# A three-layer decoder on one core: in the second layer the attention product reaches feature layout by DMA, not by TensorE transpositions

## The reference, cut to what matters

```python
x = _layernorm(x + attn(x))            # causal, 16 heads of 16 features
x = _layernorm(x + xattn(x, ctx))      # cross attention with a key mask
x = _layernorm(x + ffn(x))             # attention without mask, plus a mixture of 8 experts, 2 of them used
# in each attention: softmax(q k^T / 4) v, heads side by side; in the first two a projection W_o and a bias follow
```

## Time and profile before

| | |
|---|---|
| median of three executions | 923.28 us (922.69 to 924.7) |
| profiled execution | 925.48 us, its span 923.7 us |
| busy: PE, PEld | 94%, 80% of the span |
| busy: DVE, ACT, POOL | 84%, 63%, 46% |
| DMA | 109 GB/s mean |

### The profile page before, as it was taken

One profiled execution on the slowest core, in us unless ns is written; L12 is line 12 of the kernel. 1 busy time (PEld: TensorE's weight loads), 2 busy tenths in 40 slices (PEclk: granted clock), 3 DMA queues, 4 the chain that ended last, 5 costly groups with the idle time before them and its releaser, 6 DMA issues.

```text
span 923.7 us, 28634 instructions
## 1 busy us (share of the span) xinstructions
PE 872.9 (94%) x9988; PEld 741.6 (80%) x9988; DVE 774.2 (84%) x3718; ACT 582.9 (63%) x1211; POOL 427.7 (46%) x588
## 2 busy tenths in 40 slices
PE   7798999989889999999999999999999999999996
PEld 4688888878778888888888778888888888888874
DVE  3689898988978888888898878888888888888885
ACT  4578777877777887878787644444444444445433
POOL 7588787878775453535445323222222222222201
PEclk8999999999999999999999999999999999999999
DMA  6565565545444453444434222222222222222210
GB/s 176 158 174 166 136 174 150 158 143 166 127 111 133 114 154 95 132 113 117 118 109 112 71 71 71 82 82 82 82 81 82 82 82 82 82 81 78 66 35 24
DMA packets 98165, 100.49 MB, mean 109 GB/s; under 512 B 10701, under 2 KB 90599, under 8 KB 98023
## 3 DMA queue, kind: packets, MB, share of 16 engines
q1 hardware_dynamic: 97159, 97.87, 38.3%
q10 hardware_dynamic: 864, 0.79, 0.4%
HBM read 18.14 MB, written 4.19 MB: 24 GB/s over the span
## 4 chain that ended last, share of the span: by engine, by line
PE 71%; ACT 8%; issue 8%; DMA 5%; DVE 4%; POOL 2%; SPq 2%; ACTq 0%; POOLq 0%; DVEq 0%
PE work L517 39%; PE work L661 9%; PE scores L638 8%; PE max_scores L614 7%; DMA q_stack<-neg_max_t 4%; PE work L670 3%; PE scores L641 3%; ACT attn L827 2%; PE work L542 1%; SPq L443 1%; ACT x_all L849 1%; DVE max_scores L993 1%; ACT neg_max_t L821 1%; DMA q_stack<-q_parts 1%; PE work L704 1%
## 5 line engine op out<-in xcount | busy, mean ns | idle before, releaser
L993 DVE CUSTOM_DVE_ANT_0 max_scores<-max_scores,mask_qk 128x128 f32<-128x128 f32 x992 | 253.3, 324 | 36.1 <-PE max_scores L614 35.7
L827 ACT ACTIVATE attn<-scores 128x512 f32<-128x512 f32 x384 | 214.9, 595 | 74.2 <-PE scores L638 68.3
L638 PE MATMUL scores<-q_stack,k_stack 128*128 128x128 bf16 x1536 | 144.6, 220 | 21.8 <-DMA q_stack<-neg_max_t 10.8
L614 PE MATMUL max_scores<-k_stack,q_stack 126*128 126x128 bf16 x1536 | 148.7, 221 | 5.8 <-DMA q_stack<-q_parts 3.6
L1107 POOL TENSOR_TENSOR q_full<-q_full,q_parts 128x512 f32<-128x512 f32 x48 | 55.9, 1164 | 192.9 <-ACT q_parts L779 192.9
L993 DVE DVE_READ_ACCUMULATOR2_ANT neg_max<- 128x1 f32 x992 | 138.8, 140 | 0.0
L638 PEld LDWEIGHTS scores<-q_stack,k_stack 128*128 128x128 bf16 x1536 | 97.0, 97 | 44.1 <-DMA q_stack<-neg_max_t 17.2
L614 PEld LDWEIGHTS max_scores<-k_stack,q_stack 126*128 126x128 bf16 x1536 | 99.1, 98 | 41.4 <-issue 22.8
L1066 DVE SCALAR_TENSOR_TENSOR x_all<-work,combine,x_all 128x256 f32<-128x256 f32 x256 | 122.6, 479 | 7.5 <-PE work L517 2.8
L517 PE MATMUL work<-split_hi,w_hi 128*128 128x256 f32 x384 | 115.7, 301 | 4.5 <-DVE split_lo L896 4.4
L517 PE MATMUL work<-w_hi,split_hi 128*128 128x256 f32 (+2 forms) x320 | 113.6, 355 | 0.0
(11 more groups left out here) (125 smaller groups left out, 2073.8 us busy)
## 6 DMA issues: line engine op xcount, KB each, us to landing
q_stack<-q_parts SPq DMA_DIRECT2D x288, 128.0 KB, 2.4
k_stack<-k_parts SPq DMA_DIRECT2D x282, 128.0 KB, 2.4
in_t<-in_xt SPq DMA_DIRECT2D x16, 256.0 KB, 3.0
x_all<-in_x SPq DMA_DIRECT2D x16, 256.0 KB, 3.2
in_t<-in_ct SPq DMA_DIRECT2D x16, 256.0 KB, 2.8
out<-x_all SPq DMA_DIRECT2D x16, 256.0 KB, 2.2
stage<-in_e SPq DMA_DIRECT2D x4, 512.0 KB, 4.7
stage<-in_qk SPq DMA_DIRECT2D x2, 512.0 KB, 4.1
```

The lines of the kernel that those rows point to most:

```text
L614: mm = pe.matmul(dst[:, b, h2, :], head(QS, n, 2 * p + h2, b, ROWS), head(KS, n, 2 * p + h2, b, ROWS), start=(b + h2 == 0), stop=(b + h2 = ...
L638: mm = pe.matmul(dst[:, b, h2, :], head(KS, n, 2 * p + h2, b, rows), head(QS, n, 2 * p + h2, b, rows), start=(b + h2 == 0), stop=(b + h2 = ...
L827: act.activation(attn("exp", n, p)[:, :, :], SS[g % 2][:, :, :, :].rearrange("k b h q -> k (b h) q"), ACT.Exp).then_inc(probs_done, 1)
L993: ins = dve.tensor_tensor_reduce(scores, scores, MQ[l][:, :], -1.0, HUGE, ALU.add, ALU.min, NM[n % 2][:, b, h:h + 1])
```

## The change: what it does

In the second layer (`MOVED = (1,)`):

- `VA` holds 32 columns for each head in all layers, feature and one in turn (feature 0, one, feature 1, one, ...). So the product with v has features on the even rows and the sum on each odd row. The halves of the pairs are laid out so that a row holds 512 values that make up two rows of the feature layout.
- `zd` (SyncE, for each half f): a DMA of the 64 even rows (128 KB) into `ZC[:, f, :]`, and a DMA of one sum row for each of four heads-in-a-quad (8 KB) into `ZS[:, f, :]`, spread over 128 lanes, 16 values in each.
- `rz` (VectorE): the reciprocal of `ZS` (128 x 32) and its split in three bf16 parts, five small instructions, each waiting for the one before.
- `rd` (SyncE): three DMAs that gather each part (8 KB, 128 pieces of 64 bytes) into 8 rows of `RT`.
- `bc` (PE): two bf16 matmuls with a selecting matrix `SEL`, 24 rows deep and 256 columns wide, which spread each reciprocal over the features of its head. `z` is then one multiplication of 128 x 512 on VectorE, in place in `ZC`.
- `zT` and `zt` are gone in this layer. `zh` and `zl` read `ZC` in SBUF and not PSUM. `zd` of the next item waits for `zl`.
- The weights and biases are permuted on the host, the constants have one more load (128 KB) and one more cast, and the memset of `VA` grows from 574 to 1024 values per lane for each buffer.
- All due times of all three layers are new. The order of PE around `maxt` in the second layer is now: `s2` (seventh, eighth), `s1` (eighth), `xt`, `pv` (second half), `v`, `maxt`, `q`, `s1`, `s1`, `s2` (first), `s2`, `s1`, `k`, `s2`, `s2`, `bc`. On VectorE: `nm`, `xl`, `rz`, then the eight `max` of the next item with `cl`, `z`, `zl` and `sum` between them. On SyncE: `zd` (second half), `ml`, `rd`, then `qs`. On ScalarE `za` (second half) comes straight after the last `exp`.

```diff
-VH = DH + 1
-V_COLS = (H - 1) * VH + QUAD
+V_COLS = H * QUAD
+MOVED = (1,)
-PERIOD = [16.53, 18.13, 24.97]
+PERIOD = [16.52, 18.01, 25.02]
 ...
+     "z": [23.59], "in": [-69.69], "ch": [-49.91], "cl": [-48.7], "xt": [-41.93], "xh": [-40.53], "xl": [-38.82],
+     "res": [-0.26], "zh": [24.2], "zl": [24.69], "out": [26.33], "sum": [28.38], "rs": [35.67], "norm": [44.58],
+     "va": [-12.54], "zd": [8.35, 14.21], "rz": [17.38], "rd": [14.91], "bc": [23.06]},
 ...
+            def move_z(n, f):
+                sp.wait_ge(za_done[f], n + 1)
+                if n:
+                    sp.wait_ge(zl_done, n)
+                src = attn("za", n, f)
+                sp.dma_start(ZC[:, f, :], src[0:P:2, :, :]).then_inc(z_moved[f], 16)
+                sp.dma_start(ZS[:, f, :], src[1:P:QUAD, :, :]).then_inc(z_moved[f], 16)
+
+            def move_recips(n, part):
+                sp.wait_ge(recip_done, moved(n))
+                if moved(n) > 1:
+                    sp.wait_ge(bc_psum, moved(n) - 1)
+                for j in range(PARTS):
+                    sp.dma_start(RT[8 * j:8 * j + 8, :], RP[j][:, :, :]).then_inc(recip_moved, 16)
 ...
-                            o, h = QUAD * (2 * b + h2), 8 * f + 2 * p + h2
-                            mm = pe.matmul(dst[o:o + QUAD, p * P:(p + 1) * P], VA[n % VALUES][:, b, h * VH:h * VH + QUAD],
+                            h, half = 8 * f + 2 * p + h2, p // 2
+                            o, u = QUAD * (2 * (p % 2) + h2), 2 * half + b
+                            mm = pe.matmul(dst[o:o + QUAD, u * P:(u + 1) * P], VA[n % VALUES][:, b, h * QUAD:(h + 1) * QUAD],
 ...
+            def broadcast_recips(n, part):
+                pe.wait_ge(recip_moved, PARTS * 16 * moved(n))
+                dst = mine("bc", n)
+                recips = RT[0:8 * PARTS, :].rearrange("r (m f e) -> r m f e", f=2, e=P // 8)
+                for f in range(2):
+                    mm = pe.matmul(dst[:, f * TOK:(f + 1) * TOK], SEL[0:8 * PARTS, :], recips[:, :, f, :], start=True, stop=True)
+                mm.then_inc(bc_psum, 1)
 ...
             def z_tokens(n, f):
+                if layer(n) in MOVED:
+                    for g in range(2):
+                        dve.wait_ge(z_moved[g], 2 * 16 * moved(n))
+                    dve.wait_ge(bc_psum, moved(n))
+                    z = ZC[:, :, :].rearrange("p c t -> p (c t)")
+                    dve.tensor_tensor(z, bank("bc", n)[:, :], z, ALU.mult).then_inc(zq_done, 1)
+                    return
 ...
+            def sum_recips(n, part):
+                for g in range(2):
+                    dve.wait_ge(z_moved[g], 2 * 16 * moved(n))
+                if moved(n) > 1:
+                    dve.wait_ge(recip_moved, PARTS * 16 * (moved(n) - 1))
+                link(dve.reciprocal(ZS[:, :, :], ZS[:, :, :]))
+                for j in range(PARTS - 1):
+                    link(dve.tensor_copy(RP[j][:, :, :], ZS[:, :, :]))
+                    ins = dve.tensor_tensor((ZS if j < PARTS - 2 else RP[j + 1])[:, :, :], ZS[:, :, :], RP[j][:, :, :], ALU.subtract)
+                    if j < PARTS - 2:
+                        link(ins)
+                ins.then_inc(recip_done, 1)
 
             def z_low(n, part):
                 dve.wait_ge(zh_done, n + 1)
+                if layer(n) in MOVED:
+                    dve.tensor_tensor(ZL[:, :, :], ZC[:, :, :], ZH[:, :, :].bitcast(F32), ALU.subtract).then_inc(zl_done, 1)
+                    return
```

127 lines of the change are left out of this document (84 added, 43 removed), and 61 rows, old and new, of tables (SHIFTS, TIMES).

## The result

The changed kernel takes 946.28 us (median of four executions, 942.04 to 953.86) against 922.99 (922.07 to 924.7) before: a ratio of 1.0249, interval 1.0208 to 1.0291. Slower, as forecast, but by 23 us instead of 4, and outside the range of 914 to 939. The four executions lie at 942.0, 943.7, 948.9 and 953.9; the profiled one is that of 943.71, with a span of 941.9.

A forecast was written before the change was run, and what follows sets the result against it. PE's instructions were taken to bound the second layer; its saving would go to waits at `ml` and `rz`. 15 cycles x 0.2 us plus 0.7 for the start gave +3.7, 927.0 us from 923.28; range 914 to 939.

The forecast's parts named there:

- The usual cycle: Second layer, `maxt` to `maxt`: 16.2 us a cycle, 0.2 more than now.
- PE's wait there: PE before the first `s2`, for the DMA `ml`: stands still 0.97 us instead of 0.20.
- `bc` comes at: PE reaches `bc` about 6.8 us after `maxt`, just in time for the last `rd` DMA, landing at 6.9 (8.1).
- surplus: VectorE's `zl`, with both inputs now in SBUF: 0.15 to 0.3 us more, bounds 0 and 1.0.
- The price of `rz`: Five linked VectorE instructions on 128x32: 1.07 us, bounds 1.07 and 3.4.
- One cycle was taken for all: Sum over the second layer: 15 cycles x 0.2 us = 3 us.
- 12.7 of 16 us: SyncE's issuing in a cycle: some 8.4 us now, 12.7 with seven more issues at 0.61 each.
- Whatever is late here has no cover: PE at `bc`: at the long end of the `rd` landing, PE and VectorE lose over a microsecond once more.
- Rival C: Clearly slower: DMAs with 64-byte pieces take 3.6 us or more, `bc` late too; cycle some 17.0 us, 938 to 940; chance 0.15.
- The start: Longer `VA` memset before PE's warm-up, one more load and cast: +0.7 us, between -1 and +2.
- From the first `maxt` of the first layer to the first of the second: First layer, same instructions in a new order: 0 us, between -2 and +3.
- 3.2 + 12.7 + 0.46: VectorE's cycle: `rz` ends 3.2 us after `maxt`, 12.7 to `nm`, 0.46 for `nm` and hand-over; given as 16.3 us.

The follow-up runs named there:

- experiment 9: Changed kernel without the sums' DMAs, `rz`, `rd`, `bc` and `z`, plus idle reciprocals on VectorE before the first `max` of four items: 939.14 us.
- experiment 10: Changed kernel without sums, `rz`, `rd`, `bc`, `z`, with ScalarE's `norm` after the last `exp`: 921.28 us; additionally k earlier 930.41, or v before second `pv` 937.83.

## Why the prediction was wrong, and where it was right

- **The usual cycle, right.** 16.2 us was forecast; ten of the 15 cycles are between 15.99 and 16.93. `rz` was to end 3.2 us after `maxt`, and does at 3.20, by two errors that cancel: the sums are issued at +0.13 instead of -0.3, and are there 1.92 us later instead of 2.4. `ml` took 3.19 us from `maxt` to the first `s2` (3.17 forecast), PE's wait there is 0.59 instead of 0.97, with 0.16 more before `q`. `bc` comes at 7.06 (6.8 forecast), `zl` costs no surplus.
- **The price of `rz`, wrong, and with it the total.** This is the step that failed. The prediction had bounds of 1.07 and 3.4 us and took the low end "since the form is the same". Usual is 1.15; in three items it is 2.1 to 2.97. The form was not what mattered, but what GpSimd does at that time: the subtraction for q starts 3.76 us after `maxt`, 0.56 after `rz` is over. No step of the prediction placed `rz` against GpSimd's rows, nor asked what the missing `zt` does to ScalarE's copy of q and so to GpSimd, whose subtraction came 5.08 us after `maxt` before.
- **One cycle was taken for all.** The sum is 15 equal cycles. SyncE was reckoned at 12.7 of 16 us by the median issue, and `zd` said to be issued at -0.3. The longest stack issue took 1.99 us before as well and 1.86 after, of a median of 0.6; before it cost nothing (the one of 1.84 us at 402.7 lies in a cycle of 15.99), as nothing urgent stood behind it. Now `zd` does, and the spread went straight to VectorE. In the three long cycles the sums were issued 0.4 to 1.5 us later than in the usual one, and in one of them they landed 0.7 later besides. The line of the prediction "Whatever is late here has no cover" was right, but had no number.
- **The clock, missing.** Idle times of PE of 1.8 to 4.9 us cost another 1.0 to 1.7 us in experiment 9, by a granted clock of 0.5 to 0.8 behind them, and 1.2 us at equal idle time in experiment 10. No term and no rival had it. The long cycle from 350.63 on is 1.2 us late issue, 1.8 us collision and 1.55 us clock. In the other two the collision is 1.0 and 1.8 us, and what is left for the clock 1.5 and 2.0. The three are 14 to 15 us of the 19.3.
- **Rival C, nearest in size, wrong in mechanism.** It gave 938 to 940, 6 us short, by 64-byte pieces that land in 3.6 us in every cycle. They are used 1.92 to 2.08 us after their issue, once 2.61. *That agrees with the Trainium skill, "DMA: Bandwidth & Descriptors", "Why small descriptors are slow (HBM only)", by which copies within SBUF don't pay for short pieces; the 512 bytes of its section "Specifications" did not show.*
- **The start** took +1.7 instead of +0.7 us, within its bounds (the first `maxt` is at 34.9 to 37.9 in the traces with the new layout, so one trace says little). From the first `maxt` of the first layer to the first of the second it was 2.3 us shorter, where 0 with -2 to +3 was given: just outside. The first cycle of the second layer was another 0.9 shorter.
- **Two slips in the sums.** 3.2 + 12.7 + 0.46 is 16.4, not 16.3, and the forecast's range is given once as 925 to 931 and once as 923 to 932. Neither changes the outcome.

That the number of long cycles makes the spread of the four executions (steps of some 5 us between 943.7, 948.9 and 953.9) is likely by its size, but only one execution was traced.
